# The second layer's weights, moved out of the experts' loop

## The reference, cut to what matters

```
x   [8, 256, 512]
xn = layernorm(x)
x  = x + L0_attention(xn) + L0_experts(xn)     # 32 heads, block-wise with decay; 16 experts, 2 chosen
xn = layernorm(x)                              # the second layer begins here
x  = x + L1_attention(xn) + L1_mixture(xn)

L0_experts: y[t] = sum over 2 chosen e of gate * ((silu(x w1[e] + b1[e]) * (x w2[e] + b2[e])) w3[e] + b3[e])
L1_attention: qkv = xn Wqkv + bqkv (one head of 128);  softmax(q k^T / sqrt(128)) v;  out Wo + bo
L1_mixture: top 16 of 64 scores xn Wr^T; gates = softmax; out = sum_k gates * ((xn A_k^T) B_k) * 2
```

## Time and profile before

| | |
|---|---|
| median of 3 runs | 2654.06 us |
| the profiled execution's own time | 2654.57 us |
| its span in the trace | 2652.7 us |
| TensorE matmul busy | 2544.7 us (96%) |
| VectorE, ScalarE, GpSimd busy | 42%, 43%, 51% |
| mean granted TensorE clock | 0.986 of full speed |
| experts' loop | about 2155 to 2335 us |
| second layer | about 2335 us to the end |

### The profile page before, as it was taken

How to read it: one execution, slowest core, us unless ns; L and a number is a source line. 1 busy time by engine, 2 the same in 40 slices (tenths; PEclk the granted TensorE clock), 3 DMA queues, 4 the chain that set the end, 5 groups by cost and what they waited for, 6 DMA issues and landing times.

```text
span 2652.7 us, 40192 instructions
## 1 busy us (share of the span) xinstructions
PE 2544.7 (96%) x13674; PEld 2187.9 (82%) x13674; DVE 1118.0 (42%) x1903; ACT 1129.2 (43%) x2061; POOL 1358.2 (51%) x1357
## 2 busy tenths in 40 slices
PE   6899999999999999889999999999999989968999
PEld 5788888888888888668888888888888878857777
DVE  5433333333333334763333333333333378864553
ACT  4544444444444443434344434334434347733332
POOL 5654555555555552665555555555555368832110
PEclk9999999999999999999999999999999999989999
DMA  4211111111111111311111111111111079831110
GB/s 151 86 46 53 45 53 45 45 56 51 45 48 54 48 46 49 113 54 46 46 53 47 52 45 45 60 47 45 51 54 46 11 251 320 276 100 43 37 32 32
DMA packets 73151, 187.81 MB, mean 71 GB/s; under 512 B 12098, under 2 KB 15826, under 8 KB 73094
## 3 DMA queue, kind: packets, MB, share of 16 engines
q1 hardware_dynamic: 64550, 170.26, 18.9%
q0 software_dynamic: 8544, 16.82, 2.3%
HBM read 168.13 MB, written 26.79 MB: 73 GB/s over the span
## 4 chain that ended last, share of the span: by engine, by line
PE 84%; DVE 7%; ACT 3%; DMA 2%; issue 2%; POOL 1%; ACTq 0%; SPq 0%; DVEq 0%; POOLq 0%
PE bank L88 23%; PE bank L89 23%; PE bank L90 23%; PE bank L921 4%; PE bank L907 4%; PE bank L923 2%; PE bank L908 2%; DMA exin<-xn_rows,ecur 1%; DVE el L1981 1%; ACT eh L1949 0%; ACT exth L1940 0%; DMA l_stage<-y_slots,slot_of 0%; ACT eh L1945 0%; POOL l_stage L2485 0%; DVE ebias L1980 0%
## 5 line engine op out<-in xcount | busy, mean ns | idle before, releaser
L88 PE MATMUL bank<-xh,wh 128*128 128x512 f32 x1400 | 562.3, 402 | 23.4 <-DVE bank L1375 8.3
L90 PE MATMUL bank<-xh,wl 128*128 128x512 f32 x1400 | 548.1, 392 | 0.0
L1592 POOL TENSOR_TENSOR wl<-raw,wh 128x512 fp32r<-128x512 f32 x196 | 250.9, 1296 | 166.2 <-ACT wh L1167 163.7
L88 PEld LDWEIGHTS bank<-xh,wh 128*128 128x128 f32 x1400 | 264.8, 189 | 79.3 <-DVE bank L1375 9.2
L1406 DVE TENSOR_TENSOR acc<-bank,acc 128x512 f32<-128x512 f32 x256 | 176.8, 691 | 339.6 <-PE bank L90 339.6
L89 PE MATMUL bank<-xl_sums,wh 128*128 128x512 f32 x800 | 317.4, 397 | 0.0
L90 PEld LDWEIGHTS bank<-xh,wl 128*128 128x128 f32 x1400 | 264.2, 189 | 57.6
L88 PE MATMUL bank<-wh,xh 128*128 128x256 f32 x1024 | 293.9, 287 | 4.1 <-DVE xl L476 3.4
L90 PE MATMUL bank<-wh,xl 128*128 128x256 f32 x1024 | 291.3, 284 | 0.0
L89 PE MATMUL bank<-wl,xh 128*128 128x256 f32 x1024 | 291.1, 284 | 0.0
L1369 DVE TENSOR_TENSOR ms<-bank,dcur 128x384 f32<-128x384 f32 x256 | 142.1, 557 | 351.6 <-PE bank L908 342.5
(11 more groups left out here) (336 smaller groups left out, 5370.6 us busy)
## 6 DMA issues: line engine op xcount, KB each, us to landing
raw<-in_w_pairs_dram SPq DMA_DIRECT2D x128, 512.0 KB, 3.9
raw<-in_o_pairs_dram SPq DMA_DIRECT2D x32, 512.0 KB, 3.2
eraw<-in_ex_dram SPq DMA_DIRECT2D x31, 513.0 KB
y_slots<-ey SPq DMA_DIRECT2D x31, 512.0 KB
dcur<-in_decay_dram SPq DMA_DIRECT2D x32, 384.0 KB, 3.0
eraw<-in_ex_dram SPq DMA_DIRECT2D x31, 256.0 KB
l_raw<-in_l_w_dram SPq DMA_DIRECT2D x28, 192.0 KB
out_dram<-acc SPq DMA_DIRECT2D x16, 256.0 KB, 2.1
```

Of the source, the lines that this page charges most:

```text
L88: pe.matmul(out, wh, mh, start=start and i == 0, stop=False, skip_group_check=True)
L90: ins = pe.matmul(out, wl, mh, start=False, stop=stop and i == n - 1, skip_group_check=True)
L1592: pool.tensor_tensor(wl[:, cols], src, wh[:, cols].bitcast(F32), ALU.subtract).then_inc(w_lo, 1)
```

## The change

- In the experts' loop the pieces' loads, casts and subtractions are gone. Three large loads by SyncE bring 6400 columns straight to the place of the low parts (`w1raw` lies on `w1l`): columns 0 to 2304 before the wait of step 27, and 2048 columns each before those of steps 28 and 29.
- The biases' copy goes from VectorE to ScalarE, ahead of the casts of the first two weights.
- In the second layer 13 casts by ScalarE stand ahead of its events, 7 subtractions by VectorE ahead of its own, and 6 subtractions by GpSimd behind the gathers of group 0. They write the low part over the raw value.
- B (4096 columns) is loaded in two halves by SyncE once the second half of group 0 is normalized. ScalarE casts two of its eight parts at each of four places of group 0; GpSimd subtracts two between the two gathers of group 1 and six behind them.
- TensorE waits for each part of the weights at its first use.

```diff
         def run(r, b):                                    # routed_experts, sync
...
-            is_piece, i, _, n = tile(r, b, 2, PIECES)
-            if is_piece:
-                load_piece(i, n)
             is_tile, i, _, n = tile(r, b, 0)
             if is_tile:
+                second_layer(i)
                 sp.wait_ge(a_y, i + 1)
...
+        def second_layer(i):
+            half = (L_B - L_A) // 2
+            for step, a, b, done in ((NTILES - 4, 0, L_A, dma_wq), (NTILES - 3, L_A, L_A + half, dma_wa),
+                                     (NTILES - 2, L_A + half, L_B, dma_wa)):
+                if isinstance(i, int) and i == step:
+                    sp.dma_start(w1raw[:, a:b], l1_w[:, a:b]).then_inc(done, 16)
...
                 a.wait_ge(dma_w[n], half * 16 + 16)       # scalar
+                wait(a, v_hf, i - 1)
+                a.copy(bias[n][:], raw12[n][:, 2 * SEC:W12])
                 for j in range(2):
                     a.copy(eh[n][:, w(j)], raw12[n][:, w(j)]).then_inc(a_hi, 1)
-            is_piece, k, half_k, nk = tile(r, b, 0, PIECES)
-            if is_piece:
-                a.wait_ge(dma_l1[nk], half_k * 16 + 16)
-                a.copy(w1h[:, bass.ds(k * PIECE, PIECE)], l1raw[nk][:]).then_inc(a_l1, 1)
...
                     v.wait_ge(a_hi, i * 2 + j + 1)        # vector
-                    if j == 0:
-                        wait(v, v_hf, i - 1)
-                        v.tensor_copy(bias[n][:], raw12[n][:, 2 * SEC:W12])
...
-            is_piece, k, _, nk = tile(r, b, 0, PIECES)    # gpsimd
-            if is_piece:
-                c = bass.ds(k * PIECE, PIECE)
-                pool.wait_ge(a_l1, k + 1)
-                pool.tensor_tensor(w1l[:, c], l1raw[nk][:], w1h[:, c].bitcast(F32), ALU.subtract).then_inc(p_l1, 1)
...
+    steps = [(i * SEC, (i + 1) * SEC) for i in range(3)] + [(L_R, L_O), (L_O, L_A)]      # layer_one
+    first_a, first_b, EARLY = len(steps), len(steps) + NR, len(steps) + 2
+    steps += [(L_A + i * SEC, L_A + (i + 1) * SEC) for i in range(NR)]
+    steps += [(L_B + i * D, L_B + (i + 1) * D) for i in range(NR)]
+
+    def weights_high(a, some):
+        for i in some:
+            if i == 0:
+                a.wait_ge(dma_wq, 16)
+            if i == first_a:
+                a.wait_ge(dma_wa, 32)
+            if i == first_b:
+                a.wait_ge(q["dma_wb"], 32)
+            c = slice(*steps[i])
+            a.copy(w1h[:, c], w1raw[:, c]).then_inc(q["a_w"], 1)
+
+    def weights_low(eng, some, done):
+        for i in some:
+            c = slice(*steps[i])
+            eng.wait_ge(q["a_w"], i + 1)
+            eng.tensor_tensor(w1l[:, c], w1raw[:, c], w1h[:, c].bitcast(F32), ALU.subtract).then_inc(done, 1)
...
     def scalar(a):
+        weights_high(a, range(first_b))
         for what, g, i in events:
+            if g == 0 and (what, i) in (("route", 0), ("top", 1), ("top", 2), ("mix", 0)):
...
+                weights_high(a, range(first_b + 2 * k, first_b + 2 * k + 2))
...
     def vector(v):
+        weights_low(v, range(EARLY), q["v_w"])
...
             for i in range(CHOSEN):                       # gpsimd
                 gather(0, i, [t])
+        weights_low(pool, range(EARLY, first_b), q["p_w"])
...
                 gather(g + 1, 0)
+                if g == 0:
+                    weights_low(pool, range(first_b, first_b + 2), q["p_w"])
                 gather(g + 1, 1)
+                if g == 0:
+                    weights_low(pool, range(first_b + 2, first_b + NR), q["p_w"])
...
+        for i in range(2):                                # sync, behind the selection's loads
+            half = slice(L_B + i * (L_USED - L_B) // 2, L_B + (i + 1) * (L_USED - L_B) // 2)
+            sp.dma_start(w1raw[:, half], l1_w[:, half]).then_inc(q["dma_wb"], 16)
```

More of the change, by code:

```diff
@@ L116, in two_layers @@
                     for i, c in enumerate("hl"))
-        experts_in = (ex, l1_w, xn_dram, y_slots, ident, expert_of, token_at, table_in, w1h, w1l)
-        layer_one_in = (w1h, w1l, b_qkv, b_o, sel, ident, acc, slot_of, gate_of, y_slots, out_tiles)
+        w1raw = nc.alloc_sbuf_tensor_at("l1_raw", [P, L_ALL], F32, offset=w1_at + 4 * L_ALL)
+        experts_in = (ex, l1_w, xn_dram, y_slots, ident, expert_of, token_at, table_in, w1raw)
+        layer_one_in = (l1_w, w1raw, w1h, w1l, b_qkv, b_o, sel, ident, acc, slot_of, gate_of, y_slots, out_tiles)
         with ExitStack() as ctx:
@@ L692, in half @@
                                          lambda eng: wait(eng, pe_p, product_at(UNITS, 1, 4)))
-                layer1 = layer_one(nc, sem, xh_at, ps, *layer_one_in, experts["stored"])
+                layer1 = layer_one(nc, sem, xh_at, ps, *layer_one_in, experts["stored"], *experts["weights"])
             else:
@@ L1797, in routed_experts @@
     xth, xtl = ([x[:].rearrange("p (k s) -> p k s", k=KC) for x in some] for some in (xth, xtl))
-    l1raw = pair("l1_raw", [P, PIECE])
     s1, hf = pair("es", [P, SLOT_T]), pair("ehf", [P, SLOT_T])
@@ L1803, in routed_experts @@
     xt, hp, op = [banks[0:2], banks[2:4]], banks[4:6], ps[6:8]
-    dma_w, dma_w3, dma_x, dma_y, dma_l1 = ([sem(f"{n}{i}") for i in range(2)]
-                                           for n in ("dma_w", "dma_w3", "dma_x", "dma_y", "dma_l1"))
-    a_l1, p_l1 = sem("a_l1"), sem("p_l1")
+    dma_w, dma_w3, dma_x, dma_y = ([sem(f"{n}{i}") for i in range(2)] for n in ("dma_w", "dma_w3", "dma_x", "dma_y"))
+    dma_wq, dma_wa = sem("dma_l1_q"), sem("dma_l1_a")
     pe_xt, pe_h, pe_o, a_hi, a_hi3, a_xh, a_s, a_hh, a_y, v_lo, v_xl, v_hf, v_hl, v_y, p_lo3, p_cur, p_clear = (
@@ L2046, in routed_experts, with layer_one @@
     return {"sync": sync, "tensor": tensor, "scalar": scalar, "vector": vector, "gpsimd": gpsimd,
-            "stored": [(dma_y[b], 16 * ((NTILES + 1 - b) // 2)) for b in range(2)]}
-def layer_one(nc, new_sem, at, ps, w1h, w1l, b_qkv, b_o, sel_in, ident, acc, slot_of, gate_of, y_slots, out_tiles, stored):
+            "stored": [(dma_y[b], 16 * ((NTILES + 1 - b) // 2)) for b in range(2)], "weights": (dma_wq, dma_wa)}
+def layer_one(nc, new_sem, at, ps, l1_w, w1raw, w1h, w1l, b_qkv, b_o, sel_in, ident, acc, slot_of, gate_of, y_slots,
+              out_tiles, stored, dma_wq, dma_wa):
     end = at
@@ L2111, in layer_one, with weights_there @@
     sel_raw = [gs, hf]
+    steps = [(i * SEC, (i + 1) * SEC) for i in range(3)] + [(L_R, L_O), (L_O, L_A)]
[17 more added lines that the diff above has]
+            eng.tensor_tensor(w1l[:, c], w1raw[:, c], w1h[:, c].bitcast(F32), ALU.subtract).then_inc(done, 1)
+    def weights_there(pe, i):
+        if i < EARLY:
+            pe.wait_ge(q["v_w"], i + 1)
+        else:
+            pe.wait_ge(q["p_w"], i + 1 - EARLY)
     def rows_of(g, i, t):
@@ L2172, in outputs @@
             pe.wait_ge(q["v_hl"], NR * g + i + 1)
+            if g == 0:
+                weights_there(pe, first_b + i)
             c = slice(i * D, (i + 1) * D)
@@ L2186, in tensor @@
                     pe.wait_ge(q["v_xl"], 2 * (i // 3) + 2)
+                if i < 3:
+                    weights_there(pe, i)
                 bank = fill(hb, h_fill, h_taken, (what, g, i))
@@ L2195, in tensor @@
             if what == "hid":
+                if g == 0:
+                    weights_there(pe, first_a + i)
                 bank = fill(hb, h_fill, h_taken, (what, g, i))
@@ L2215, in tensor @@
             if what == "scores_t":
+                if g == 0:
+                    weights_there(pe, 3)
                 parts = [(wr[0][:, k * K1:(k + 1) * K1], wr[1][:, k * K1:(k + 1) * K1], xh[g % 2][:, k, :],
@@ L2261, in tensor @@
                     pe.wait_ge(q["v_ol"], g + 1)
+                    if g == 0:
+                        weights_there(pe, 4)
                     for t in range(TPG):
@@ L2279, in scalar @@
     def scalar(a):
+        weights_high(a, range(first_b))
         for what, g, i in events:
+            if g == 0 and (what, i) in (("route", 0), ("top", 1), ("top", 2), ("mix", 0)):
+                k = [("route", 0), ("top", 1), ("top", 2), ("mix", 0)].index((what, i))
+                weights_high(a, range(first_b + 2 * k, first_b + 2 * k + 2))
             if what == "stats":
```

4 lines of the change are left out of this document (2 added, 2 removed).

## The result

The changed kernel takes 2673.09 us, the median of 4 runs (2672.23 to 2673.81); the kernel before takes 2653.72 us beside it on the same chip. The ratio is 1.0071, with a 95% interval of 1.0058 to 1.0085: 19 us slower, where I forecast 2654.7 and a range that ended at 2661.5. The profiled execution took 2672.38 us; its span is 2670.4 us, 17.7 us more than before.

A forecast was written before the change was run, and what follows sets the result against it. TensorE was 96% busy; quiet loop steps were taken as bound by a ring of ScalarE, GpSimd and VectorE waits, full tiles by DMA bytes. Loop -7.5 and losses +8.2 gave +0.7 us: 2654.7 us, range 2646 to 2661.5.

The forecast's parts named there:

- The bound of the loop: Experts' loop: quiet steps set by a chain of waits through ScalarE, GpSimd and VectorE, 5.56 us falling to 5.43.
- The ring through GpSimd's subtraction: Quiet steps: VectorE's subtractions stay held behind GpSimd's, so moving the bias copy gains 0.13 us a step, 3.6 us over 28.
- nothing by themselves in a quiet step: Experts' loop, quiet steps: removing the pieces' cast and subtraction gains nothing; the pieces cost only bytes.
- So of the lost 5.4 us I take 3.9 as gained: Full tiles of the loop: fewer bytes at 337 GB/s win back 3.9 us, bounds 0 and 5.4.
- rival D: Gathers' waits stay in full tiles, loop gives 3.6 us at most, second layer costs 10: 2660.5 us; chance 0.22.
- Its second half, 10 us: Second layer in the slower rival: beginning paid in full, 8.2 us up to 11, taken as 10.
- I take +0.5 (0 to 1): End of the loop: the last store lands later because of the large loads, 0.5 us lost, bounds 0 to 1.
- each instruction ... waits for one subtraction: Second layer, VectorE beside GpSimd's subtractions: held over one each, losing 4.9, 1.15 and 1.65 us at three places.
- my term began with L78: Second layer's beginning: VectorE's delays counted from L78, due at 2348.90 and ending at 2350.0; 4.9 us in all.
- If L78 shows 0.16 us, my price of the beginning is wrong: Sign for the second layer's beginning: L78 was expected to take about 1.2 us beside GpSimd's six subtractions.
- 7.7, all six: Second layer's beginning: upper bound of the loss, all six GpSimd subtractions on the chain; 4.9 us was taken.
- The balance: Whole kernel: loop gains 7.5 us, second layer with the last store loses 8.2, sum +0.7 us.

The follow-up runs named there:

- run 5: The kernel before with one edit, the biases' copy moved to ScalarE: 2653.54 us, ratio 1.0004.
- run 6: The changed kernel with the biases' copy back on VectorE, the pieces still out of the loop: 2675.95 us, ratio 1.0081.
- run 8: The changed kernel with its large loads cut into 28 of 128x384, one per loop step, splitting still in the second layer: 2673.34 us, ratio 1.0074.
- run 9: The changed kernel with all 14 second-layer low parts on VectorE and the loop's gathers issued ahead of GpSimd's third-weight subtraction: 2644.0 us, ratio 0.9952.
- run 10: The changed kernel with all low parts on VectorE, gathers ahead of GpSimd's subtraction, and 28 loads of 128x384 in the loop: 2641.49 us, ratio 0.9947.
- Run 1: The changed kernel with the six GpSimd subtractions at the second layer's beginning given to VectorE: 2667.07 us, ratio 1.0048.
- run 2: The changed kernel with GpSimd waiting for each of its 14 second-layer subtractions to complete before issuing the next: 2668.03 us, ratio 1.0043.
- run 7: The kernel before with GpSimd issuing gathers ahead of its third-weight subtraction, one small instruction ahead of them: 2658.1 us, ratio 1.0014.
- run 12: The changed kernel with gathers first, 28 loads in the loop and all low parts on VectorE, its subtractions spread over more places: 2649.49 us, ratio 0.9978.

## Why the prediction was wrong

*The bound of the loop: half right.* The ring through GpSimd's subtraction was right in kind: the pair of VectorE's subtractions ends 1.16 us behind GpSimd's (1.09 forecast). Its price was not: the biases gave 0.06 us a quiet step for 0.13 [runs 5, 6]. Quiet steps fell to 5.36 us all the same, 5.43 forecast, since "nothing by themselves in a quiet step" was wrong for the pieces: 0.14 us each. Two errors of opposite sign made that figure look near.

*"So of the lost 5.4 us I take 3.9 as gained": failed.* It gained nothing. The term took 337 GB/s as the limit of the transfers; it was only what happened to be moved. The late steps of the full tiles are set by a ring of GpSimd's queue and the gathers' landing, 12.24 us for the two steps shown, and taking the pieces' bytes out left it as it was (runs 6 and 8 against before and after). Issuing the gathers earlier, with more bytes a second, ended it (runs 9 and 10). My own rival D had the gathers' waits staying ("if a gather lands late ... and not because of the mean rate"), with 0.22, though it blamed bursts of loads and not the place of the issue; its loop term, 3.6 us at most, came to 2.9 over the 28 steps. Its second half, 10 us, was too small for the same reason as the forecast's. The chain of waits of before had said it: 6.36 us for one gather, with the gathers' issue standing behind a subtraction.

*"I take +0.5 (0 to 1)" for the last store: mis-sized.* 3.0 us, shown by run 8, which loads otherwise and has none of it. I had let the late load and the stores share the rate; the third load was issued at 2326.28, ahead of the last two stores, and landed only at about 2334.4, just before ScalarE's casts go on.

*"each instruction ... waits for one subtraction": failed, and the dearest step.* 4.9 us were forecast and 7.7 measured; 1.15 and 2.45; 1.65 and 5.8, the last beyond even my bound of 4. The rows that I had at 1117.47 show instructions that slip in between GpSimd's subtractions, and I took it for the rule. In the three rows of weight subtractions of the changed kernel none slips in: the instruction ends with the whole row. Run 1 shows that the row is the cause, run 2 that a semaphore wait between its instructions lets VectorE in. What separates a row that shuts VectorE out from one that does not is open. It is not the distance of GpSimd's starts. The pair at 2383.27 took 2.56 us and shut VectorE out; elsewhere in the same trace a pair takes 2.49 us, and an instruction of VectorE that began with it is through after the first of the two:

```profile
1152.04 2.49 POOL L1594 TENSOR_TENSOR wl<-raw,wh 128x512 fp32r<-128x512 f32 x2 [0.73 <-ACT wh L1169]
1152.06 1.28 DVE L255 CAST slot_of<-acc 128x16 int32<-128x16 f32 x1
```

In all three rows that shut it out the held instruction had begun ahead of the row, by 0.44, 0.02 and 0.16 us. That doesn't settle it either, since run 7's low part began 0.57 us behind the first of two subtractions and was held over both. And my term began with L78: L2362 (L2399 after), whose start stands 0.44 us ahead of the row, was counted as free, and is the very one that was held. My sign "If L78 shows 0.16 us, my price of the beginning is wrong" came true, but with the price too low and not too high. The bound for the first place, "7.7, all six", was the true value; the value that I took was the one that the single pattern gave, at all three places.

The Trainium skill, "SBUF — State Buffer" (Who interferes with whom), says of VectorE's modes with two ports that the one that issues first has the shared pair "for the whole instruction" and the other waits. Run 2 agrees as to the length (1.75 us at most for a small instruction). In the changed kernel 7.82 us passed beside six instructions, and the held one had the earlier recorded start, so the measurement decides: a hold can last over a whole row.

*The clock: left out.* The second and the third stop of TensorE are followed by stretches at a lower granted clock than before (0.83 for 1.00 and 0.60 for 0.83): 1.65 us in the attention's products, and most of the last 1.8, some 3 us in all. No term of mine had it.

*The balance.* Forecast -7.5 and +8.2; measured -4.2 (-2.9 in the steps that the forecast summed) and +21.9.

## What to carry to other kernels

A GpSimd instruction that reads SBUF can cost more than its own length, up to that of the row it stands in: before moving several of them behind one another, look for VectorE instructions on the critical chain beside the row, and take the whole of its length as the price to be ruled out. If a wait is for a DMA that an in-order queue issues, follow the ring from issue to landing before taking the byte rate for the limit; here moving two gathers ahead of one subtraction, with the second layer's low parts on VectorE, took the loop from 5.87 to 5.20 us a step and the kernel from 2655.63 to 2641.49 us. And work that fits into idle time by its sum can still collide by its place, so read what is late right behind each place.

## What the runs showed of the hardware that was not expected

- A VectorE instruction of 128x2 elements took 7.82 us beside six GpSimd subtractions without a wait between them, and 1.75 us with one; three additions of 128x512 took 9.47 and 4.60 us. In the same kernel other rows let VectorE in without such a wait (1152.04).
- DMA moved 394 GB/s over 20 us (run 10), with a share of 1.03 of the engines' time and full steps of 5.20 us in the mean, where 337 had looked like the top.
- The same loop settled into one of two phases, 5.14 or 5.34 us a quiet step (runs 10 and 12), with GpSimd's subtraction starting behind VectorE's pair in the one and ahead of it in the other.
